# Two graph-attention layers: aggregate product split in three passes from the fourth pair on, prologue reordered, softmax row transposed as a full block

## The reference, cut to what is computed

```python
# layer 0
q, k = split(X @ Wqk); v = X @ Wv
agg = adj @ (k * mask)
w   = mask / 16 * sum(q * agg, axis=-1)
x   = layernorm(x + softmax(w, axis=nodes)[:, :, None] * v)
# layer 1
query, keyt, value = x @ Wq.T + bq, x @ Wk.T + bk, x @ Wv.T + bv
weight = adj * exp(query @ keyt.T)
x   = layernorm(x + (weight / weight.sum(-1)) @ value)
```

## Time and profile before

| | |
|---|---|
| median of 3 runs | 321.32 us (320.49 to 321.69) |
| the profiled execution's own time | 320.88 us |
| its span, first to last instruction | 319.0 us |
| TensorE matmul busy | 303.7 us (95%), 1898 records |
| TensorE weight load busy | 271.3 us (85%) |
| VectorE busy | 221.3 us (69%) |
| ScalarE busy | 200.4 us (63%) |
| GpSimd busy | 141.7 us (44%) |
| DMA queues | 31.0% of 16 engines' span |

### The profile page before, as it was taken

One profiled execution on the slowest core, in us unless ns is written; L12 is line 12 of the kernel. 1 busy time (PEld: TensorE's weight loads), 2 busy tenths in 40 slices (PEclk: granted clock), 3 DMA queues, 4 the chain that ended last, 5 costly groups with the idle time before them and its releaser, 6 DMA issues. The chain is left out here.

```text
span 319.0 us, 6523 instructions
## 1 busy us (share of the span) xinstructions
PE 303.7 (95%) x1898; PEld 271.3 (85%) x1898; DVE 221.3 (69%) x689; ACT 200.4 (63%) x456; POOL 141.7 (44%) x177
## 2 busy tenths in 40 slices
PE   8979999999999999999999999999999999999770
PEld 6758898889998988899989888999898889998660
DVE  1476777777767787777777877777778777767652
ACT  3445556667666666676666666766666667665562
POOL 1355553334555544345555344455553344553312
PEclk9999999999999999999999999999999999999997
DMA  7820223222333332323333332223333322110002
GB/s 247 296 66 36 82 85 115 86 82 84 100 115 115 115 114 83 82 87 94 115 115 115 115 87 78 83 98 115 115 115 115 91 73 82 66 53 34 33 35 99
DMA packets 19021, 31.26 MB, mean 98 GB/s; under 512 B 2112, under 2 KB 6336, under 8 KB 19008
## 3 DMA queue, kind: packets, MB, share of 16 engines
q1 hardware_dynamic: 19008, 31.11, 31.0%
HBM read 22.71 MB, written 8.39 MB: 97 GB/s over the span
## 5 line engine op out<-in xcount | busy, mean ns | idle before, releaser
L258 POOL TENSOR_TENSOR rstd<-var_eps,minus_half 128x4 f32<-128x4 f32 x35 | 35.6, 1017 | 157.6 <-ACT x L315 86.0
L315 ACT ACTIVATE x<-x_sum,shift,rstd 128x256 f32<-128x256 f32 x64 | 35.0, 594 | 48.6 <-POOL shift L261 48.6
L522 PE MATMUL ps<-w_hi,xt_hi 128*128 128x512 f32 x128 | 61.6, 482 | 0.4 <-DVE w_lo L511 0.3
L524 PE MATMUL ps<-w_hi,xt_lo 128*128 128x512 f32 x128 | 50.3, 393 | 0.0
L523 PE MATMUL ps<-w_lo,xt_hi 128*128 128x512 f32 x128 | 50.2, 392 | 0.0
L282 POOL TENSOR_TENSOR x1b<-x,bv_all 128x512 f32<-128x512 f32 x32 | 41.3, 1289 | 2.4 <-ACT x L315 2.4
L266 POOL TENSOR_TENSOR xt_lo<-xt_raw,xt_hi 128x512 fp32r<-128x512 f32 x31 | 40.0, 1290 | 4.8 <-ACT xt_hi L309 4.8
L522 PE MATMUL ps<-wv_hi,x1t_hi 128*128 128x258 f32 x128 | 38.9, 304 | 0.0
L362 ACT ACTIVATE z<-ps,z_bias 128x256 f32<-128x256 f32 x64 | 26.8, 470 | 16.3 <-PE ps L524 16.3
L315 ACT ACTIVATE x<-x,shift,rstd 128x256 f32<-128x256 f32 x64 | 34.9, 594 | 3.2 <-POOL shift L261 3.2
L394 DVE CUSTOM_DVE_ANT_0 agg<-ps,agg,adjt 128x256 f32<-128x256 f32 x64 | 31.0, 484 | 8.3 <-issue 5.7
(11 more groups left out here) (77 smaller groups left out, 646.0 us busy)
## 6 DMA issues: line engine op xcount, KB each, us to landing
xt_raw<-xt_pairs SPq DMA_DIRECT2D x32, 256.0 KB, 2.8
x_raw<-x_pairs SPq DMA_DIRECT2D x32, 256.0 KB, 2.7
out_pairs<-x SPq DMA_DIRECT2D x32, 256.0 KB, 2.0
adjt<-adjt_pairs SPq DMA_DIRECT2D x32, 129.0 KB, 2.1
p<-params SPq DMA_DIRECT2D x1, 770.0 KB, 6.8
p<-params SPq DMA_DIRECT2D x1, 512.0 KB, 3.8
p<-params SPq DMA_DIRECT2D x1, 256.0 KB, 4.8
bv_all<-value_bias SPq DMA_DIRECT2D x1, 128.0 KB, 7.5
```

The costliest lines, as they stand in the source:

```text
L258: nc.gpsimd.tensor_tensor(rstd[r % 2][:, :, :], var_eps[:, :, :], minus_half[:, :, :], ALU.pow)\
L315: last = nc.scalar.activation(out[:, graph(g)], in_[:, graph(g)], ACT.Identity, bias=shift[r % 2][:, layer, g:g + 1], scale=rstd[r % 2][:, ...
L522: nc.tensor.matmul(out, s_hi, m_hi, start=first, stop=False)
L524: return nc.tensor.matmul(out, s_lo, m_hi, start=False, stop=last)
```

## The change

- **Aggregate.** From pair 3 on (`SPLIT = 3`), `aggregate` is a split product of three passes per graph in place of one fp32 matmul. ScalarE gets two casts in each slot, `split_adjm(t+3)` (128x256, behind the x1 norm and ahead of the z copy) and `split_x(t+4)` (128x512, at the slot's end). GpSimd gets two subtractions, `low_x(t+3)` (128x512, at the head of the slot, ahead of `rstd`) and `low_adjm(t+3)` (128x256, behind `xt_lo`, ahead of `x1b`). `mask_adj(t+3)` moves from the slot's end to right behind `shift`. `aggregate` then waits for the low parts.
- **Softmax row.** `p_row` becomes a 128x128 tile, zeroed once; `transpose_p` transposes all of it against the full identity into `[:, 1, 0:128]`, of which two columns are read as before.
- **Prologue.** Warm-up is 8 matmuls on the zeroed `p_row`, which need no identity. `m0`'s second half is split after both halves of `wv0`. `aggregate(0)` moves between the two halves of `project(0, 0)`. `aggregate(2)` moves from slot 0 to ahead of `transpose_w(1)`. In slot 0 `project(2, 0)` comes ahead of `transpose_p(1)`. GpSimd masks pairs 1 and 2 in slot -2, and `wv1_lo` moves to slot -1, between `xt_lo(2)` and `x1b(0)`.

```diff
+SPLIT = 3
-WARM_UP = 7
+WARM_UP = 8
-        p_row = sb("p_row", [2, 128])
+        p_row = sb("p_row", [128, 128])
...
 # gpsimd
+            def low_adjm(u, r):
+                pool.wait_ge(adjm_hi_done, u + 1 - SPLIT)
+                nc.gpsimd.tensor_tensor(adjm_lo[r % 2][:, :], adjm[r % 2][:, :],
+                                        adjm_hi[r % 2][:, :].bitcast(F32), ALU.subtract).then_inc(adjm_lo_done, 1)
+            def low_x(u, r):
+                pool.wait_ge(x_hi_done, u + 1 - SPLIT)
+                nc.gpsimd.tensor_tensor(x_lo[r % 2][:, :], x_raw[r % 4][:, :],
+                                        x_hi[r % 2][:, :].bitcast(F32), ALU.subtract).then_inc(x_lo_done, 1)
             def slot(t, r):
+                if exists(t + 3) and r + 3 >= SPLIT:
+                    low_x(t + 3, r + 3)
...
+                if exists(t + 3) and r + 3 >= SPLIT:
+                    mask_adj(t + 3, r + 3)
...
                 if r == -2:
-                    mask_adj(t + 3, r + 3)
+                    mask_adj(1, 1)
+                    mask_adj(2, 2)
+                if r == -1:
                     pool.wait_ge(wv1_hi_done, 1)
...
+                if exists(t + 3) and r + 3 >= SPLIT:
+                    low_adjm(t + 3, r + 3)
...
-                if exists(t + 3) and r != -2:
-                    mask_adj(t + 3, r + 3)
...
 # scalar
+            def split_x(u, r):
+                act.wait_ge(x_loaded[r % 4], transfers4(u, r))
+                act.wait_ge(agg_done, u - 1)
+                nc.scalar.copy(x_hi[r % 2][:, :], x_raw[r % 4][:, :]).then_inc(x_hi_done, 1)
+            def split_adjm(u, r):
+                act.wait_ge(adjm_done, u + 1)
+                act.wait_ge(agg_done, u - 1)
+                nc.scalar.copy(adjm_hi[r % 2][:, :], adjm[r % 2][:, :]).then_inc(adjm_hi_done, 1)
...
                     norm(x1[(r + 1) % 2], x1_sum[(r + 1) % 2], 0, r, x1_done)
+                if exists(t + 3) and r + 3 >= SPLIT:
+                    split_adjm(t + 3, r + 3)
...
                     nc.scalar.copy(val[:, :, 0:DIM], val_ps[:, :, 0:DIM]).then_inc(val_copied, 1)
+                if exists(t + 4) and r + 4 >= SPLIT:
+                    split_x(t + 4, r + 4)
...
 # tensor, aggregate
+                    else:
+                        mm = split_product(agg_ps[:, g, :], [(adjm_hi[r % 2][:, n], adjm_lo[r % 2][:, n],
+                                                              x_hi[r % 2][:, graph(g)], x_lo[r % 2][:, graph(g)])])
...
-                nc.tensor.transpose(p_col_ps(r), p_row[:, :], ident[0:2, 0:2]).then_inc(p_col_done, 1)
+                nc.tensor.transpose(p_full_ps(r), p_row[:, :], ident[:, :]).then_inc(p_col_done, 1)
...
                 if exists(t + 2):
-                    aggregate(t + 2, r + 2)
+                    if r > 0:
+                        aggregate(t + 2, r + 2)
+                    project(t + 2, r + 2, 0)
                 if r == 0:
                     transpose_p(1, 1)
-                if exists(t + 2):
-                    project(t + 2, r + 2, 0)
...
-            project(0, 0, 0)
+            pe.wait_ge(first_xt_lo_done, 1)
+            project_half(0, 0, 0, 0)
             aggregate(0, 0)
-            project(0, 0, 1)
+            project_half(0, 0, 0, 1).then_inc(yv_done[0], 1)
+            project_half(0, 0, 1, 0)
+            project_half(0, 0, 1, 1).then_inc(yv_done[1], 1)
...
             project(1, 1, 1)
+            aggregate(2, 2)
             transpose_w(1, 1)
```

More of the change, by code:

```diff
@@ L73, in build @@
         adjm = [sb(f"adjm{i}", [128, PAIR_N]) for i in range(2)]
+        x_hi = [sb(f"x_hi{i}", [128, PAIR_X], F32R) for i in range(2)]
+        x_lo = [sb(f"x_lo{i}", [128, PAIR_X], F32R) for i in range(2)]
+        adjm_hi = [sb(f"adjm_hi{i}", [128, PAIR_N], F32R) for i in range(2)]
+        adjm_lo = [sb(f"adjm_lo{i}", [128, PAIR_N], F32R) for i in range(2)]
         agg = sb("agg", [128, 2, DIM])
@@ L120, in build @@
         ident_zeroed, ident_ready, consts_ready = sem("ident_zeroed"), sem("ident_ready"), sem("consts_ready")
+        p_row_zeroed = sem("p_row_zeroed")
         bq_widened = sem("bq_widened")
@@ L140, in build @@
         first_xt_lo_done = sem("first_xt_lo_done")
+        x_hi_done, x_lo_done, adjm_hi_done, adjm_lo_done = sem("x_hi_done"), sem("x_lo_done"), sem("adjm_hi_done"), sem("adjm_lo_done")
         xt_lo_done, adjm_done, x1b_done = sem("xt_lo_done"), sem("adjm_done"), sem("x1b_done")
@@ L166, in w_row_ps, with p_full_ps @@
             return yv_ps(r)[0:2, 0, 0:NODES]
+        def p_full_ps(r):
+            return yv_ps(r)[:, 1, 0:NODES]
         def p_col_ps(r):
-            return yv_ps(r)[:, 1, 0:2]
+            return p_full_ps(r)[:, 0:2]
         def norms(t):
@@ L285, in slot @@
                         bv_all[:, :].unsqueeze(1).broadcast_to([128, 2, DIM]), ALU.add).then_inc(x1b_done, 1)
-                if exists(t + 3) and r != -2:
-                    mask_adj(t + 3, r + 3)
+            nc.gpsimd.memset(p_row[:, :], 0.0).then_inc(p_row_zeroed, 1)
             nc.gpsimd.memset(ident[:, :], 0.0).then_inc(ident_zeroed, 1)
@@ L376, in slot @@
                     nc.scalar.copy(val[:, :, 0:DIM], val_ps[:, :, 0:DIM]).then_inc(val_copied, 1)
+                if exists(t + 4) and r + 4 >= SPLIT:
+                    split_x(t + 4, r + 4)
             split_xt(0, 0)
+            act.wait_ge(m0_done, 1)
+            nc.scalar.activation(w0_hi[:, 0, 0:DIM], m0_ps[:, 0, :], ACT.Copy, scale=ATT_SCALE).then_inc(m0_hi_done, 1)
+            act.wait_ge(wv0_loaded, 16)
             for m in range(HALVES):
-                act.wait_ge(m0_done, m + 1)
-                nc.scalar.activation(w0_hi[:, m, 0:DIM], m0_ps[:, m, :], ACT.Copy, scale=ATT_SCALE).then_inc(m0_hi_done, 1)
-                act.wait_ge(wv0_loaded, 16)
                 nc.scalar.copy(w0_hi[:, m, DIM:2 * DIM], wv0[:, m, :]).then_inc(wv0_hi_done, 1)
+            act.wait_ge(m0_done, HALVES)
+            nc.scalar.activation(w0_hi[:, 1, 0:DIM], m0_ps[:, 1, :], ACT.Copy, scale=ATT_SCALE).then_inc(m0_hi_done, 1)
             slots(act, slot)
@@ L490, in slot @@
                         dve.wait_ge(p_col_done, t + 2)
-                    nc.vector.tensor_scalar(p_row[:, :], exp_row[:, :], inv_sum[:, 0:1], None, ALU.mult)\
+                    nc.vector.tensor_scalar(p_row[0:2, :], exp_row[:, :], inv_sum[:, 0:1], None, ALU.mult)\
                         .then_inc(p_row_done, 1)
@@ L504, in _, with low_m0 @@
                 .then_inc(first_xt_lo_done, 1)
-            for m in range(HALVES):
+            def low_m0(m):
                 dve.wait_ge(m0_hi_done, m + 1)
@@ L509, in _ @@
                     in1=w0_hi[:, m, 0:DIM].bitcast(F32), op0=ALU.mult, op1=ALU.subtract).then_inc(m0_lo_done, 1)
+            low_m0(0)
+            for m in range(HALVES):
                 dve.wait_ge(wv0_hi_done, m + 1)
@@ L512, in _ @@
                                         ALU.subtract).then_inc(wv0_lo_done, 1)
+            low_m0(1)
             dve.wait_ge(params1_loaded, 16)
@@ L516, in _ @@
             dve.wait_ge(ident_ready, 1)
+            dve.wait_ge(consts_ready, 1)
             slots(dve, slot)
@@ L532, in aggregate @@
             def aggregate(u, r):
-                pe.wait_ge(adjm_done, u + 1)
-                pe.wait_ge(x_loaded[r % 4], transfers4(u, r))
+                if r < SPLIT:
+                    pe.wait_ge(adjm_done, u + 1)
+                    pe.wait_ge(x_loaded[r % 4], transfers4(u, r))
+                else:
+                    pe.wait_ge(adjm_lo_done, u + 1 - SPLIT)
+                    pe.wait_ge(x_lo_done, u + 1 - SPLIT)
                 if exists(u - 1):
@@ L538, in aggregate, with project_half @@
                 for g in range(2):
-                    mm = nc.tensor.matmul(agg_ps[:, g, :], adjm[r % 2][:, graph(g, NODES)], x_raw[r % 4][:, graph(g)],
-                                          start=True, stop=True)
-                mm.then_inc(agg_done, 1)
+                    n = graph(g, NODES)
+                    if r < SPLIT:
+                        mm = nc.tensor.matmul(agg_ps[:, g, :], adjm[r % 2][:, n], x_raw[r % 4][:, graph(g)],
+                                              start=True, stop=True)
+                    else:
+                        mm = split_product(agg_ps[:, g, :], [(adjm_hi[r % 2][:, n], adjm_lo[r % 2][:, n],
+                                                              x_hi[r % 2][:, graph(g)], x_lo[r % 2][:, graph(g)])])
+                mm.then_inc(agg_done, 1)
+            def project_half(u, r, g, k):
+                if r == 0:
+                    pe.wait_ge(m0_lo_done, k + 1)
+                    pe.wait_ge(wv0_lo_done, k + 1)
+                return split_half(yv_ps(r)[:, g, :], xt_hi[r % 2][:, k, g, :], xt_lo[r % 2][:, k, g, :],
+                                  w0_hi[:, k, :], w0_lo[:, k, :], k == 0, k == HALVES - 1)
             def project(u, r, g):
-                if r == 0:
-                    pe.wait_ge(first_xt_lo_done, 1)
```

(7 more changed lines are left out.)

## The result

The changed kernel took 324.82 us (median of 4 runs, 324.40 to 325.03) against 321.50 us of the kernel before beside it: ratio 1.012, 95% interval 1.0096 to 1.0135. It is 1.2% slower. The forecast was 320.0 with a range of 309.5 to 323.5, so the time lies above the range. Its profiled execution took 324.69 us, with a span of 322.8.

What follows compares the result with a forecast made beforehand. TensorE bounds the kernel at 9.11 us a slot. From the profiled 320.88: prologue +0.7, 28 periods -1.4, a maskless period -0.33, last `transpose_p` -0.2, together -1.2: 319.7; the median stands 0.44 higher: 320.0, range 309.5 to 323.5.

Steps and rivals of the forecast that it cites:

- The bound: TensorE bounds the old kernel; in the changed one the loop through GpSimd's `x1b` and `p_row` does, chance 0.72.
- Aggregate, 0.15 a slot: Six split passes on TensorE take 0.71 us where the fp32 aggregate takes 0.87, a gain of 0.15 a slot.
- transpose, 0.19: The full-block `transpose_p` takes 0.11 us of TensorE's time where the small one takes 0.30, a gain of 0.19 a slot.
- The loop's length, 9.06: From `p_col` through `shift`, four GpSimd instructions to `x1b`'s end, and `p_row`, back to `p_col`: 9.06 us against 9.11.
- 28 periods x -0.05 = -1.4: The sum's term for the repeated slots: each period 0.05 us shorter, together 1.4 us off.
- each tenth is a tenth a slot: `low_x` ends 0.1 to 0.4 us before `edge` and `x1t_hi`; without that margin each tenth costs a tenth a slot.
- a gain of 0.05 +/- 0.10: Gain per slot with its spread, from the two new instruction lengths and the late transpose.
- Prologue, +0.7: Start-up ahead of the steady slots: 0.7 us slower, taken between +0.2 (row alone) and +1.3 (with the two-input rule).
- TensorE as the bound: Rival: `p_row` gets through, for instance because asked for before `x1b` starts, and TensorE stays the bound: 309.8 us, chance 0.15.
- The full block leaves the hole: Rival: the full transpose keeps TensorE's hole at `transpose_p`; 315.3 us if TensorE is the bound, chance 0.05.
- `p_row` loses twice: Rival: behind `x1b`, `p_row` also waits for GpSimd's `low_x`, 1.3 us more a slot: 357 us, chance 0.06.
- Covers: Added or moved work elsewhere, such as casts, the earlier mask, later `x1b`, `low_x` and loads, fits in without cost.

Runs made afterwards that it cites:

- e1: The changed kernel with the softmax's exponentials written to PSUM, so that `p_row` reads PSUM instead of SBUF: 313.36 us, 0.977 of the kernel before.
- e4: The changed kernel with GpSimd's `x1b` ahead of `low_adjm` instead of behind it: 314.17 us, 0.980 of the kernel before.
- e5: The changed kernel with the hardware loop unrolled eight times instead of four, so two jumps back instead of five: 322.90 us, 1.005 of the kernel before.
- e2: The changed kernel with the aggregate left fp32, without the four splitting instructions, mask at the slot's end; full-block transpose and new prologue stay: 315.69 us, 0.985 of the kernel before.
- e3: The changed kernel with `p_row` transposed as 2 rows against a 2x2 identity, as before: 324.41 us, 1.013 of the kernel before.

## Why the prediction was right or wrong

**The bound (right).** TensorE bound the kernel before, the loop through `p_row` binds the changed one. L536's mean is 0.93 us (forecast near 1.1), its end 0.08 behind `x1b`'s. e1 and e4, which undo this overlap by two different ways and keep the added work, take 11.5 and 10.7 us off.

**Aggregate, 0.15 a slot, and transpose, 0.19 (right in size).** 0.15 and 0.17, both unseen in the changed kernel, both seen in e1.

**The loop's length, 9.06 (wrong, and this decided the sign).** The step that failed is "28 periods x -0.05 = -1.4", which takes one length of the loop for all slots. Measured: 258.32 - 28 x 9.11 = +3.2, against the kernel before, an error of 4.6 us, which is nearly all of 324.69 - 319.7 = 5.0 (0.14 more is the prologue's; the end gained 0.20 where 0.53 was forecast). It has two parts.

- *The plain slot was mis-sized by 0.05.* It is 9.11, not 9.06, and so equal to the old one: 1.4 us over 28 slots. `low_adjm` was priced at 0.62 like the mask of the same shape and takes 0.74, 0.12 more; the other terms came out 0.07 shorter together. In a plain slot the loop is 4.80 from `p_col` to `shift`'s end, 3.75 to `x1b`'s end, 0.08, and 0.48 to the next `p_col`; the forecast has 4.88, 3.65, 0.08 and 0.45.
- *The jump was left out.* The sum treated 28 slots as alike, since in the kernel before they are. That evenness was itself a product of TensorE's being the bound. Five jumps back and the entry into the loop add the rest, 258.32 - 28 x 9.11 = 3.2 us. e5 takes three of the five jumps away and 1.6 us of the 28 periods with them (9.228 to 9.172 a period). The 3.2 us have three sources. GpSimd's later `rstd`, 3 x 0.08 at the entry and at each jump, is 6 x 0.24 = 1.4. TensorE's late transposes, which put VectorE's cast back by 0.15 at each jump, are 0.8. The third is an overlap: after a late slot the next is late too, because `x_lo` is released later, lies over `edge` at the next slot's start and holds it, for 0.19 five times and for 0.08 behind the entry, 1.0 in all. The forecast named this as "each tenth is a tenth a slot" and did not price it. VectorE and GpSimd at the start of the second slot behind a jump, where `edge` takes 0.60 us, and `edge` in a slot where it is free, 0.41:

```profile
142.42 1.30 POOL L267 TENSOR_TENSOR x_lo<-x_raw,x_hi 128x512 fp32r<-128x512 f32 x1 [0.64 <-ACT x_hi L343]
...
143.39 0.60 DVE L476 TENSOR_TENSOR edge<-exp_s,adjt 128x256 f32<-128x256 f32 x1
...
152.76 0.41 DVE L476 TENSOR_TENSOR edge<-exp_s,adjt 128x256 f32<-128x256 f32 x1
```

So the spread given for a slot, a gain of 0.05 +/- 0.10, did not hold the mean, a loss of 0.11 against the old period, although it held the plain slot.

**Prologue, +0.7 (right in size, in part by luck).** The third `transpose_p` came 0.84 later (31.50 against 30.66). The Trainium skill (SBUF — State Buffer, "Who interferes with whom") says that a VectorE instruction with two inputs in SBUF contends with a GpSimd instruction that reads SBUF; the trace agrees, with 1.65 us for `x1t_lo` beside `x_lo` against 0.69. The forecast went half way between that rule (+1.3) and a trace that had no such row (+0.2). The hold came nearly in full, 0.96 of the 1.1 that the forecast gave it by that rule, and without it the prologue would stand at 0.84 - 0.96 = -0.12, not at +0.2. So the full rule held, the rest of the prologue gained 0.3 more than forecast, and a middle value that was a hedge came out close.

**Rivals.** TensorE as the bound (309.8 forecast) is what e1 gives, at 313.4: the difference is the prologue, which e1 does not mend, and the jumps. "The full block leaves the hole" falls by e2. "`p_row` loses twice" falls by e4, by the cast in slot 0 and by the changed kernel itself: at the third `transpose_p`, `x_lo` is issued at 31.21, before `x1b` ends at 31.27, and `p_row`, waiting since 30.25, ends at 31.35. At a change-over between two GpSimd instructions a VectorE instruction that already waits goes first if it was issued early enough. The row at 29.77 is no freak: it was issued 0.1 us before `x1b`'s end and lost, and so did `p_row` in e2 at 29.09 (0.08 before the end, 0.72 us long) and in e3 at 20.48 (0.09, 1.42 us). Every one that was issued 0.19 us or more before the end went first. What happens in between, and why 0.1 us is too late, no run settles. In the changed kernel `p_row` is issued 0.70 us or more before `x1b`'s end.

**Covers (right but for one).** Loads, ScalarE's 1.0 us a slot and GpSimd's 2.0 us a slot cost nothing by themselves, as e1's plain slots of 8.79 show. The one that failed is the margin of `low_x` ahead of `edge`, above.

## What to carry to other kernels

Before GpSimd gets more work, list the VectorE instructions that read SBUF in the closing link of the loop (here a cast, a tensor_scalar and tensor_tensors with two SBUF inputs) and ask which GpSimd instruction will lie over each: not the share of busy time but this overlap decided here, and it can be removed by reading from PSUM or by swapping two instructions. When a saving on the bound engine makes it wait for another, costs return that its backlog had hidden, here those of the loop's jump on TensorE and on GpSimd; evenness of the periods before is no evidence that they are free. And price a shape by an instruction of the same operand form: the mask with its broadcast operand was 0.12 us shorter than the subtraction of the same size.

## What the runs showed of the hardware that was not expected

- A full 128x128 fp32 transpose at the end of a stream of matmuls costs TensorE 0.17 us less than one with 2 rows and 2 columns (8.94 against 9.11 us a slot, e2).
- Behind a jump of a hardware loop, TensorE's next matmuls came 0.72 to 0.76 us after the end of the instruction that it had waited for last (changed kernel, e1 to e4), against 0.28 without a jump (changed kernel).
- In the three slots behind the loop's entry and behind each jump, GpSimd's `rstd` starts 0.32 us after the start of VectorE's `var_eps`, for which it waits, and 0.24 in all others (changed kernel; e5 moves it with the jumps).
- A held VectorE instruction gets in between two GpSimd instructions that are issued back to back if it was issued 0.19 us or more before the first one's end; at 0.08 to 0.10 it waited for the second too (before, e2, e3). A GpSimd instruction that it overtakes with a long cast takes longer (`x_lo` 1.48 us at 22.07, where 1.29 is usual); behind the short `p_row` of e4 `adjm_lo` keeps its 0.73.
- With its input in PSUM the same `tensor_scalar` takes 0.34 us, beside GpSimd or not; from SBUF it takes 0.27 alone and up to 1.42 beside GpSimd (e3).
